# Edges per node: three products of ones on TensorE, or one product of a sum made on GpSimd

## What is computed

```python
for r in range(weight.shape[0]):
    mask = (edge_type == r).astype(x.dtype)
    sums = segment_sum(msgs * mask[:, None], dst, num_segments=n)
    cnt = segment_sum(mask, dst, num_segments=n)
    mean = sums / jnp.maximum(cnt, 1.0)[:, None]
    out = out + mean @ weight[r]
```

## Time and profile before

| | |
|---|---|
| time, median of 3 runs (lowest to highest) | 1002.43 us (1002.11 to 1002.71) |
| time of the profiled execution | 1003.57 us |
| its span, first to last instruction | 1001.8 us |
| busy: TensorE products | 937.8 us (94%), 4743 instructions |
| busy: TensorE weight loads | 827.4 us (83%) |
| busy: VectorE | 617.0 us (62%) |
| busy: ScalarE | 369.2 us (37%) |
| busy: GpSimd | 469.2 us (47%) |
| mean granted clock of TensorE | 0.971 |
| products of ones (L631), all | 30, of 0.33 us each by their own records |

### The profile page before, as it was taken

One profiled execution on the slowest core, in us unless ns is written; L12 is line 12 of the kernel. 1 busy time (PEld: TensorE's weight loads), 2 busy tenths in 40 slices (PEclk: granted clock), 3 DMA queues, 4 the chain that ended last, 5 costly groups with the idle time before them and its releaser, 6 DMA issues.

```text
span 1001.8 us, 13654 instructions
## 1 busy us (share of the span) xinstructions
PE 937.8 (94%) x4743; PEld 827.4 (83%) x4743; DVE 617.0 (62%) x1000; ACT 369.2 (37%) x583; POOL 469.2 (47%) x414
## 2 busy tenths in 40 slices
PE   4999999998995979999999999999999969999994
PEld 3999999996885968888888888888888848878883
DVE  5898888876881345655556555565547465445625
ACT  6333333346882344222222222222234334234311
POOL 5344445456665303647566475654759003215322
PEclk9999999998997979999999999999999979999997
DMA  7998765542344443454435444343433513332301
GB/s 200 218 269 228 208 157 160 149 103 17 49 64 125 122 163 116 116 143 123 140 105 160 141 124 139 105 158 88 119 112 126 180 55 108 123 106 86 125 22 63
DMA packets 89794, 128.06 MB, mean 128 GB/s; under 512 B 34488, under 2 KB 67472, under 8 KB 89744
## 3 DMA queue, kind: packets, MB, share of 16 engines
q1 hardware_dynamic: 72640, 123.02, 40.8%
q0 software_dynamic: 15584, 0.11, 3.6%
q10 hardware_dynamic: 1520, 4.30, 1.2%
HBM read 116.65 MB, written 7.59 MB: 124 GB/s over the span
## 4 chain that ended last, share of the span: by engine, by line
PE 90%; DVE 4%; issue 2%; ACT 2%; DMA 1%; SPq 1%; DVEq 0%; ACTq 0%
PE ps L596 49%; PE ps L433 22%; PE ps L643 8%; PE ps L538 3%; PE ps L511 2%; PE ps L499 2%; PE ps L410 1%; DVE stats L1056 1%; DMA raw<-in_L_gnn_wq 1%; PE ps L421 1%; PE ps L747 1%; PE ps L631 1%; ACT h L769 1%; SPq L307 0%; DVE shift L1070 0%
## 5 line engine op out<-in xcount | busy, mean ns | idle before, releaser
L1180 DVE TENSOR_TENSOR wlo<-raw,whi 128x1024 fp32r<-128x1024 f32 x120 | 207.3, 1731 | 136.6 <-ACT whi L832 136.4
L433 PE MATMUL ps<-acts,whi 128*128 128x384 f32 (+1 forms) x896 | 232.4, 340 | 5.9 <-POOL wlo L1486 5.6
L1552 POOL TENSOR_TENSOR mean_lo<-mean_f,mean_hi 128x384 fp32r<-128x384 f32 x80 | 92.4, 1155 | 192.5 <-ACT mean_hi L975 192.5
L433 PEld LDWEIGHTS ps<-acts,whi 128*128 128x128 f32 x896 | 164.1, 191 | 6.4 <-issue 5.8
L975 ACT ACTIVATE mean_hi<-mean_f 128x384 fp32r<-128x384 f32 x80 | 42.0, 525 | 299.0 <-DVE mean_f L1310 299.0
L433 PE MATMUL ps<-acts,wlo 128*128 128x384 f32 (+1 forms) x448 | 151.5, 338 | 0.0
L596 PE MATMUL ps<-whi,mean_hi 128*128 128x512 f32 x480 | 149.4, 392 | 0.0
L596 PE MATMUL ps<-whi,mean_lo 128*128 128x512 f32 x480 | 148.8, 391 | 0.0
L596 PE MATMUL ps<-wlo,mean_hi 128*128 128x512 f32 x480 | 148.6, 391 | 0.0
L832 ACT ACTIVATE whi<-raw 128x1024 fp32r<-128x1024 f32 x120 | 125.4, 1049 | 21.7 <-PE ps L596 21.7
L1573 POOL DMA_INDIRECT weight_d<-weight_sum,cell x48 | 96.2, 2004 | 28.5 <-DMA weight_d<-weight_sum,cell 19.4
(11 more groups left out here) (177 smaller groups left out, 1464.4 us busy)
## 6 DMA issues: line engine op xcount, KB each, us to landing
raw<-in_L_gnn_weight SPq DMA_DIRECT2D x64, 512.0 KB
rows_b<-rows_d SPq DMA_DIRECT2D x24, 384.0 KB, 4.5
raw<-in_L_gnn_w_gate SPq DMA_DIRECT2D x16, 512.0 KB
raw<-in_L_gnn_W_self SPq DMA_DIRECT2D x16, 512.0 KB
raw<-in_L_gnn_W_neigh SPq DMA_DIRECT2D x16, 512.0 KB
count_d<-total_r SPq DMA_DIRECT2D x8, 576.0 KB
rel_r<-count_d SPq DMA_DIRECT2D x8, 576.0 KB, 4.8
raw<-in_L_gnn_wq SPq DMA_DIRECT2D x32, 128.0 KB
```

Source lines behind the costliest of these rows:

```text
L433: mm = pe.matmul(ps[:, j % 2, 0:N], stationary[j % RING][:, k, :], acts[:, a, moving, k, :], start=i == 0, stop=i == 3 * KT - 1)
L1180: dve.tensor_tensor(wlo_row[slot], raw[slot][:, :], whi_row[slot].bitcast(F32), ALU.subtract)\
L1552: pool.tensor_tensor(mean[1][:, k % 2, :], mean_f[:, k % 2, :], mean[0][:, k % 2, :].bitcast(F32), ALU.subtract).then_inc(S["mean_lo"], 1)
```

## The change

GpSimd adds the three thirds of a plane (or of `total_r`) into one tile of 128x384, `planes`, with two additions, and TensorE multiplies the ones by that tile alone: one product instead of three. The tile `cnt` is gone, `planes` has its place; VectorE writes the counts into `inv` and inverts them there, and for that waits also until its own earlier reads of `inv` are done. A new signal `planes_made` goes from GpSimd to TensorE. The first sum is made before GpSimd's first `mean_low`, those of relations 1 to 7 in step 5 of the relation before, behind the indirect transfer of that step, and that of `total_r` in step 5 of relation 7; it serves both mean layers. A sum waits for its plane and for the previous product of ones, which read `planes`.

```diff
@@ tiles, signals @@
-            cnt = sb("cnt", [P, N], F32, scope)
+            planes = sb("planes", [P, N], F32R, scope)
@@ start_relation (TensorE) @@
                 ready()
-                for s in range(NT):
-                    mm = pe.matmul(ps[:, 6, 0:N], ones_r[:, :], edges[:, s, :], start=s == 0, stop=s == NT - 1)
+                pe.wait_ge(S["planes_made"], R + 1 if isinstance(q, int) and q > R else q + 1)
+                mm = pe.matmul(ps[:, 6, 0:N], ones_r[:, :], planes[:, :], start=True, stop=True)
@@ read_counts (VectorE) @@
                 dve.wait_ge(S["agg_ready"], q * (KT + 1) + 1)
-                dve.tensor_scalar(cnt[:, :], ps[:, 6, 0:N], 1.0, None, ALU.max).then_inc(S["agg_read"], 1)
+                need(dve, S["agg_read"], q * (KT + 1))
+                dve.tensor_scalar(inv[:, :], ps[:, 6, 0:N], 1.0, None, ALU.max).then_inc(S["agg_read"], 1)
                 dve.wait_ge(S["agg_read"], q * (KT + 1) + 1)
-                dve.reciprocal(inv[:, :], cnt[:, :]).then_inc(S["inv_made"], 1)
+                dve.reciprocal(inv[:, :], inv[:, :]).then_inc(S["inv_made"], 1)
@@ GpSimd @@
+            def sum_planes(q, counts):
+
+                if q:
+                    pool.wait_ge(S["agg_ready"], (q - 1) * (KT + 1) + 1)
+                link(pool.tensor_tensor(planes[:, :], counts[:, 0, :].bitcast(F32), counts[:, 1, :].bitcast(F32), ALU.add))
+                pool.tensor_tensor(planes[:, :], planes[:, :].bitcast(F32), counts[:, 2, :].bitcast(F32), ALU.add)\
+                    .then_inc(S["planes_made"], 1)
+
             row_parts(0)
+            pool.wait_ge(rel_in[0], 16)
+            sum_planes(0, rel_r[:, 0, :, :])
@@ GpSimd, in the loop over relations r and steps k, behind add_weights @@
+                    if k == KT - 3 and r + 1 < R:
+                        pool.wait_ge(rel_in[(r + 1) % 2], 16 * ((r + 1) // 2 + 1))
+                        sum_planes(r + 1, rel_r[:, (r + 1) % 2, :, :])
+                    if k == KT - 3 and r + 1 == R:
+                        pool.wait_ge(S["total_made"], NT * (R + 1))
+                        sum_planes(R, total_r)
```

More of the change, by code:

```diff
@@ L182, in build @@
             mid_ready x_based x_done w3_hi w3_lo out_based out_psum out_done
-            vec_chain pool_chain sum_ready inv_made held_vec held_pool""".split()
+            vec_chain pool_chain sum_ready planes_made inv_made held_vec held_pool""".split()
         S = {n: sem(n) for n in names}
```

## The result

| | before | after |
|---|---|---|
| median (lowest to highest) of 8 runs | 1002.01 us (999.7 to 1002.71) | 998.06 us (996.72 to 1000.95) |
| ratio, 95% interval | | 0.9967 (0.9954 to 0.9979) |
| time and span of the profiled execution | 1003.57 and 1001.8 us | 997.92 and 996.2 us |
| products of ones (L631) | 30 | 10 |
| GpSimd busy | 469.2 us | 482.8 us |

The ratio is a gain of 3.3 us, between 2.1 and 4.6. Forecast were 3.15 us and 999.3 us. The two traces differ by more, 5.6 us of span; where the rest of that lies is told at the experiments, and the like of it is seen between two traces of the same kernel.

The account below looks back on a forecast made before the run. TensorE was taken to bound the kernel, every product in the relations being on the path. Removed products (-3.5 us) and a loss in the last relation (+0.35 us) gave -3.15 us: 999.3 us against the median of 1002.43, range 998.4 to 1001.0.

Parts of the forecast that it names:

- What bounds the kernel: TensorE, 90% of the span; in the relations every product is on the path, so starts count, not durations.
- Size of the gain: Two of three products of ones go in ten places, 0.175 us each by starts: 3.5 us, all on the path.
- GpSimd's additions: Two additions of 128x384, nine times, 1.01 us each plus 0.1 us wait between them: 2.1 us.
- wlo: VectorE's subtraction at L1180, held up beside GpSimd's additions: ends 1.10 us behind mean_lo, about 1.9 us long.
- The register wait: VectorE's added wait for its own last reading of inv, in the counts' chain: 0.04 to 0.2 us, taken as 0.07.
- The slack: From the end of the counts' chain (mean_lo) to TensorE's load of those weights: 0.27 less 0.05 us signalling, 0.22 us.
- The last relation: Sums of the total delay mean_lo of tile 7; TensorE's 13th product after them is late, 0.35 us once.
- Rival A: Counts' chain makes mean_lo of tile 0 up to 0.2 us late in seven relations, 1.4 us; 1000.7 us; chance 0.14.
- Rival B: Additions take 1.57 us each, delaying wlo and counts; loss once the pair exceeds 2.6 us; 1004.7 us; chance 0.06.
- The sum: Removed products and the last relation's loss together: -3.5 + 0.35 = -3.15 us, giving 999.3 us.

Follow-up runs that it names:

- e4: The kernel before with six products of ones instead of three in each of the ten places; ratio to the kernel before 1.0079.
- e2: The kernel before with one product of ones over the first third only, nothing added on GpSimd; ratio to the kernel before 0.9977.
- e9: The kernel before without GpSimd's 48 indirect transfers of edge weights in the relations, signals kept; one run, openings 41.87 us apart.
- e3: The changed kernel with TensorE's three products back; GpSimd's sums still made and waited for, but unread; ratio to the kernel before 1.0001.
- e7: The changed kernel with VectorE's reading of the counts done twice, once into an unread tile; ratio to the kernel before 0.9987.
- e1: The changed kernel with the sum of total_r moved from step 5 of the last relation to behind the loop; ratio to the kernel before 0.9967.
- e6: The changed kernel with the first addition of each sum made twice, three additions instead of two; ratio to the kernel before 0.9997.
- e8: The changed kernel with total_r's sum behind the loop and the second mean layer's counts not made again; ratio to the kernel before 0.9960.
- e5: The changed kernel with both additions of each sum made twice; ratio to the kernel before 1.0107.

## Why the prediction was right

**What bounds the kernel** was read rightly: what left TensorE in the relations left the time, opening by opening.

**Size of the gain.** 0.175 us a product, from starts; measured 0.173 (e4) and 0.174 (e2). 2 x 0.173 x 7 = 2.42 us against 2.39 measured between the first and the eighth group.

**GpSimd's additions** at 1.01 us and 0.1 between them: 2.14 us measured, 2.1 taken. Right. The reason holds in part: those of the earlier trace rows are long because neighbours overlap, as said, but an addition of 2.0 us is one that waited for a wlo (e9, all 24 of L1562), which the prediction did not say. Nothing else moved in the relations (e3).

**wlo** was put at an end 1.10 us behind mean_lo and came 1.09 behind it; "about 1.9 us long" was 1.70.

**The register wait** was taken at 0.07 us. There is none to be seen: the counts are read 0.03 us behind the product (0.04 before). The forecast's sum did not rest on it.

**The slack** of 0.22 us was 0.24 by the time lost and 0.32 by the product's start (e7). That it comes out so near is in part luck: the load follows the end of mean_lo by 0.13 us and not by 0.05, and a load that is 0.31 us late makes its product only 0.15 us late.

**The last relation** was named as the one place of loss, at the 13th product, 0.35 us. The wait is there, and 0.35 us is what the first product is late; with the slower spacing behind it the loss is 0.45 (e1) to 0.48 us (e3). That term was short by 0.1 us.

**Rival A** did not occur: no wait on mean_lo in an opening, in either trace of the changed kernel, and openings of 41.53 us.

**Rival B** had a wrong step. "It decides from 2.6 us on", because wlo waits for everything that stands on GpSimd, is refuted by e6: at 3.2 us nothing is lost in openings 3 to 7. I had generalised from the earlier trace rows, where wlo waits for two operations; e9 and e8 show that to be so only behind an indirect transfer and where the second operation does not wait for the first. The forecast didn't hang on it, as the additions took 2.1 us. What did stay unnamed among the rivals is the queue ahead of the sum: an indirect transfer that is issued late carries the sum with it (0.64 us of wait once in e8).

**The sum.** -2.29 us in the two stretches of the table, -0.3 for the first mean layer's opening (80.18 to 79.87) and some -0.35 for the second's, which lies behind the tenth start, give about -2.95, against -3.15 forecast and -3.3 (-4.6 to -2.1) over all runs. That all runs come within 0.15 us of the forecast is luck, as their interval is 2.5 us wide; what bears it out are the stretches. The prediction's remark that this kernel's runs differ by 0.6 us came from three runs; 28 of them spread over 5.3 us. The traces' own 5.6 us would have misled: they hold a start that moves by 1 to 2 us.

## What to carry to other kernels

Price an instruction that is taken out of a busy TensorE by the distance of starts, not by its record, which here was twice as long. Before work goes to an engine with idle time, look for the place where it will stand in that engine's queue: behind it, who waits next (here the last mean of the last relation), and ahead of it, what may come late (here scattered transfers). Compare two traces by stretches that both repeat, not by their spans.

## What was not expected of the hardware

GpSimd and VectorE took turns, one operation each, where GpSimd's operations followed each other with a start 0.03 to 0.05 us before the last end, or 0.1 us behind it (e5, e6, e9, the changed kernel). Behind an indirect transfer the records of GpSimd's next operations start 0.3 to 0.6 us before the one ahead has ended, and a VectorE subtraction with two SBUF inputs waited for both, 3.8 us instead of 1.2. In e8 the second addition waited for the first, and there the subtraction came in between even behind a transfer.

After the same short pause of TensorE between the two mean layers, the granted clock over 20 us was 0.91 in one execution of the kernel before and 1.00 in another, and the block behind the pause took 5.99 and 4.38 us. The first had 1.4 us less in a stretch before it.
